# Row maxima of attention: own keys' banks through ScalarE and GpSimd, the maxima's row last in a first score, and the attention output rounded two tiles ahead

## The reference

```python
h = layernorm(x) * (1 + ca) + sa
q = rmsnorm(h @ wq_a.T, q_a_ln_w) @ wq_b.T                  # 32 heads, 64 plain + 64 rotary
ckv, k_pe = h @ wkv_a.T                                      # latent of 32, one rotary key for all heads
k, v = from rmsnorm(ckv) @ wkv_b.T
attn = softmax(where(causal, (q . k) * scale, min))          # 1024 x 1024, causal
x = x + ga * ((attn @ v) @ wo.T)
h = layernorm(x) * (1 + cb) + sb
x = x + gb * ((silu(h @ gate_w.T * s) * (h @ up_w.T * s)) @ down_w.T * s)
```

## Time and profile before

| | |
|---|---|
| median of 3 runs (range) | 802.64 us (801.94 to 804.55) |
| the profiled execution's own time | 803.38 us |
| its span, first to last instruction | 801.60 us |
| mean granted TensorE clock | 0.993 of 2.4 GHz |
| busy: PE, weight loads, DVE, ACT, POOL | 756.7, 494.5, 555.4, 275.2, 156.3 us |
| one of the windows 0 to 5 | 60.9 us each, 6 of them |

### The profile page before, as it was taken

One profiled execution on the slowest core, in us unless ns is written; L12 is line 12 of the kernel. 1 busy time (PEld: TensorE's weight loads), 2 busy tenths in 40 slices (PEclk: granted clock), 3 DMA queues, 4 the chain that ended last, 5 costly groups with the idle time before them and its releaser, 6 DMA issues.

```text
span 801.6 us, 10308 instructions
## 1 busy us (share of the span) xinstructions
PE 756.7 (94%) x3901; PEld 494.5 (62%) x3901; DVE 555.4 (69%) x831; ACT 275.2 (34%) x394; POOL 156.3 (19%) x134
## 2 busy tenths in 40 slices
PE   3898899999999999999999999999799999999998
PEld 1755465555555555565565556545487888887886
DVE  6878579889889889879879878689567323322342
ACT  3732134333333433433333333434344322222210
POOL 1135413113114114114114100022143000000111
PEclk9999899999999999999999999999999999999999
DMA  8433513213213213123123082152100132200011
GB/s 308 159 79 80 133 42 79 65 32 79 55 41 80 49 47 79 42 54 79 35 61 80 15 287 120 59 206 82 51 0 27 51 108 79 73 11 0 27 40 39
DMA packets 36288, 60.72 MB, mean 76 GB/s; under 512 B 4272, under 2 KB 16560, under 8 KB 34448
## 3 DMA queue, kind: packets, MB, share of 16 engines
q1 hardware_dynamic: 36240, 60.06, 26.9%
HBM read 32.66 MB, written 2.10 MB: 43 GB/s over the span
## 4 chain that ended last, share of the span: by engine, by line
PE 58%; DVE 31%; issue 6%; ACT 2%; POOL 2%; DMA 1%; SPq 0%; DVEq 0%; ACTq 0%; POOLq 0%
PE PS L799 15%; DVE PR L1323 8%; PE PS L816 7%; DVE NMa L1226 7%; PE PS L636 5%; PE PS L699 5%; PE PS L714 4%; PE PS L761 4%; PE PS L700 4%; PE PS L701 4%; DVE NMb L1226 3%; DVE wide L1323 3%; PE PS L652 2%; PE PS L626 1%; PE PS L703 1%
## 5 line engine op out<-in xcount | busy, mean ns | idle before, releaser
L965 ACT ACTIVATE PR<-PS 128x1024 f32<-128x1024 f32 (+1 forms) x144 | 132.9, 929 | 259.6 <-PE PS L701 232.3
L1226 DVE TENSOR_REDUCE NMa<-PS 128x1 f32<-128x512 f32 (+3 forms) x216 | 137.8, 660 | 34.3 <-PE PS L640 30.9
L636 PE MATMUL PS<-KH,Q 96*128 96x512 f32 (+3 forms) x384 | 130.6, 400 | 3.5 <-DVE TQ L1211 1.5
L699 PE MATMUL PS<-Q,KH 97*128 97x512 f32 x288 | 130.7, 454 | 0.0
L1323 DVE TENSOR_TENSOR PR<-PR 128x2048 f32<-128x2048 f32 (+3 forms) x56 | 112.5, 2009 | 6.9 <-ACT PR L965 5.5
L700 PE MATMUL PS<-Q,KL 96*128 96x512 f32 x288 | 114.2, 396 | 0.0
L701 PE MATMUL PS<-Q,KH 96*128 96x512 f32 x288 | 113.6, 395 | 0.0
L636 PEld LDWEIGHTS PS<-KH,Q 96*128 96x128 f32 x384 | 67.7, 191 | 56.0 <-issue 29.2
L714 PE MATMUL PS<-PR,V 128*32 128x512 f32 (+3 forms) x704 | 70.4, 488 | 1.7 <-ACT PR L965 1.7
L699 PEld LDWEIGHTS PS<-Q,KH 97*128 97x128 f32 x288 | 55.9, 194 | 25.6 <-issue 13.7
L1441 DVE SCALAR_TENSOR_TENSOR wide<-PS,ffn_s,TQ 128x1024 f32<-128x1024 f32 x10 | 12.8, 1283 | 71.9 <-PE PS L799 71.9
(11 more groups left out here) (185 smaller groups left out, 1060.1 us busy)
## 6 DMA issues: line engine op xcount, KB each, us to landing
Q<-TQ SPq DMA_DIRECT2D x64, 384.0 KB, 5.5
RT<-in_wo SPq DMA_DIRECT2D x4, 1024.0 KB, 4.8
TQ<-in_wo SPq DMA_DIRECT2D x4, 1024.0 KB, 5.8
WI<-in_gate_w SPq DMA_DIRECT2D x10, 256.0 KB, 3.4
WI<-in_up_w SPq DMA_DIRECT2D x10, 256.0 KB, 3.9
DI<-in_down_w SPq DMA_DIRECT2D x10, 256.0 KB, 2.7
PR<-in_wmod_c SPq DMA_DIRECT2D x2, 1024.0 KB, 6.9
x_in<-in_x SPq DMA_DIRECT2D x8, 256.0 KB, 9.7
```

Source lines behind the costliest of these rows:

```text
L636: ins = pe.matmul(bank[:, i * w:(i + 1) * w], M.Q[0:KR, g % 2, 0, qt // 4, h0 + i, qs], M.KH[0:KR, lo:lo + w], start=(i == 0), stop=(i == ...
L699: pe.matmul(dst, M.KH[0:KR + 1, ks], M.Q[0:KR + 1, w % 2, 0, qb, :, qs], start=True, stop=False)
L965: act.activation(tiles, banks, ACT.Exp).then_inc(S_.p, 1)
L1226: dve.tensor_reduce(dst, PS[:, bank_of(turn), 0:n * w].rearrange("p (h k) -> p h k", k=w), axis=AX.X, op=ALU.max, negate=True).then_inc(S_ ...
```

## The change

1. **Own keys' banks.** Of each query tile `qt`, the 128 keys of its own tile (the diagonal block) become a part of their own: 4 heads x 128 columns in one bank. ACT copies it to `diag` in SBUF and frees the bank, POOL sets the masked entries with `affine_select`, and DVE reduces it from SBUF into NMd (`diagonal_reduced`), placed at least three parts behind. The mask matmuls L640 are gone. There are still 38 parts a group: 30 over earlier keys and 8 own ones. `join` takes two minima; it stands two units earlier than `rows` in the windows' table.
2. **First score.** In the first unit of a window the matmul with the maxima's row is issued last, and the wait for the transfer stands ahead of it alone.
3. **Rotary sum in place** (RE is now RT rows 0 and 3), so that the next half's first product waits for `split_low` (`tl`) where it waited for the sum (`re`). WV has a buffer of its own.
4. **Rounding.** AL is made by DVE for all tiles; tiles 0 and 1 after the last add, tile `st + 2` behind the gate of tile `st`. The term with AL comes last, and the first term of tile 1 is issued ahead of the last of tile 0. Four of the modulation columns move out of window 7, to DVE's queue behind the last inverted sums. ACT loads the square root's table ahead.
5. **Last output tile.** Both halves of the last residual are added by DVE.
6. **Group 0.** `FIRST_MAXIMA` puts one piece of group 1's queries behind each own-keys part.

```diff
+    for qt in (3, 2, 1, 4, 5, 6, 7):
+        for lo in range(0, qt * P, 512):
+            w = min(512, qt * P - lo)
...
+        qt = len(parts) - 1 - k
+        if qt < NS and k >= 2 + qt * (len(earlier) - 5) / NS:
+            parts.append((qt, qt * P, P, 0, HG))
```

```diff
-        if diagonal:
-            corner = bank[:, 0:n * w].rearrange("p (h k) -> p h k", k=w)[:, :, w - P:]
-            ins = pe.matmul(corner, M.identb[:], M.maskb[:].unsqueeze(1).broadcast_to([P, n, P]), start=False, stop=True)
...
+    def diagonal_copied(g, k):
...
+        if NS * g + qt >= 2:
+            act.wait_ge(S_.dm, NS * g + qt - 1)
+        act.wait_ge(S_.side, turn + 1)
+        act.activation(M.diag[:, qt % 2].rearrange("p h k -> p (h k)"), PS[:, bank_of(turn), :], ACT.Copy).then_inc(
+            S_.free[turn % 3], 1)
...
+    def diagonal_reduced(g, qt):
+        dve.wait_ge(S_.ds, NS * g + qt + 1)
+        dve.tensor_reduce(M.NMd[:, qt // 4, :, qt % 4], M.diag[:, qt % 2], axis=AX.X, op=ALU.max,
+                          negate=True).then_inc(S_.dm, 1)
...
+        pool.wait_ge(S_.free[TURN[("part", g, k)] % 3], freed(("part", g, k)))
+        pool.affine_select(out=tile, in_=tile, compare_op=ALU.is_ge, fill=MASKED, base=0, pattern=[[0, HG], [-1, P]],
+                           channel_multiplier=1).then_inc(S_.ds, 1)
...
+        dve.tensor_tensor(M.NMj[:], M.NMa[:], M.NMd[:], ALU.min).then_inc(S_.nm, 1)
```

```diff
-        if s == 0 and i == 0:
-            pe.wait_ge(S_.nd, 16 * (w + 1))
...
+        if first:
+
+            pe.wait_ge(S_.nd, 16 * (w + 1))
+            ins = pe.matmul(dst, M.KH[0:KR + 1, ks], M.Q[0:KR + 1, w % 2, 0, qb, :, qs], start=False, stop=True)
```

```diff
-            pe.wait_ge(S_.al, st + 1)
+            pe.wait_ge(S_.ah, st + 1)
...
-        a, w = ((M.AH, M.MH), (M.AL, M.MH), (M.AH, M.ML))[n]
+        if n == 2:
+            pe.wait_ge(S_.al, st + 1)
+        a, w = ((M.AH, M.MH), (M.AH, M.ML), (M.AL, M.MH))[n]
...
+    product_term(1, 0)
...
+    attn_low(0)
+    attn_low(1)
     sums_copied(G - 1, 1)
     invert(G - 1, 1)
-    dve.wait_ge(S_.al, 2)
+    for d in range(KD):
+        mod_late(3, d)
     for st in range(NS - 1):
-        if 2 <= st + 1:
-            attn_low(st + 1)
         gated(st)
+        if st + 2 < NS:
+            attn_low(st + 2)
```

More of the change, by code:

```diff
@@ L333 @@
 SLACK = 0.04
+LEAST_BEHIND = 3
 def maxima_places(begin, end):
-    cost = [0.14 + w * n / 960 for _, _, w, _, n in PARTS]
-    places = [(begin + (end - begin) * sum(cost[:k]) / sum(cost), ("part", k), cost[k]) for k in range(len(PARTS))]
-    return places + [(end + 0.02, ("join",), 0.1), (end + 0.07, ("rows",), 0.3)]
+    cost = [0.35 if is_diagonal(k) else 0.14 + PARTS[k][2] * PARTS[k][4] / 960 for k in range(len(PARTS))]
+    diagonals = [k for k in range(len(PARTS)) if is_diagonal(k)]
+    at = lambda k: begin + (end - begin) * sum(cost[:k]) / sum(cost)
+    places = []
+    for k in range(len(PARTS)):
+        for qt, d in enumerate(diagonals):
+            if k == min(d + LEAST_BEHIND + 1, (diagonals + [len(PARTS)] * 2)[qt + 2]):
+                places.append((at(k), ("least", qt), 0.65))
+        places.append((at(k), ("part", k), 0.0 if is_diagonal(k) else cost[k]))
+    return places + [(end + 0.02, ("join",), 0.1), (end + 0.12, ("rows",), 0.3)]
 def group_places(g, places):
@@ L396 @@
 FIRST_MAXIMA = [("modrow", 0, 1)]
-FIRST_MAXIMA += [key for _, key, _ in sorted(group_places(0, maxima_places(0.04, 0.84)) + group_places(1, QUERY_PLACES),
-                                             key=lambda x: x[0])]
+HANDED_PIECES = [piece for hf in range(2)
+                 for piece in ([("even", 1, hf)], [("odd", 1, hf)], [("lat", 1, hf), ("sum", 1, hf)], [("split", 1, hf)])]
+for key in [key for _, key, _ in sorted(group_places(0, maxima_places(0.0, 0.9)), key=lambda x: x[0])]:
+    FIRST_MAXIMA.append(key)
+    if key == ("part", 0, 1):
+        FIRST_MAXIMA.append(("w", 1))
+    if key[0] == "part" and is_diagonal(key[2]):
+        FIRST_MAXIMA += HANDED_PIECES[PARTS[key[2]][0]]
 BANKED = ("w", "even", "odd", "lat", "part", "rows", "den", "fold", "modrow")
@@ L537, in sp_program @@
         sp.dma_start(out[st * P:(st + 1) * P, :], M.OT[:, st % 2]).then_inc(S_.st[st % 2], 16)
[L539 to L543, removed]
+    for half in range(2):
+        cols = slice(half * D // 2, (half + 1) * D // 2)
+        sp.wait_ge(S_.oh, half + 1)
+        sp.dma_start(out[(NS - 1) * P:NS * P, cols], M.OT[:, 1, cols]).then_inc(S_.st[1], 16)
     sp.wait_ge(S_.nd, 16 * G)
@@ L645, in maxima_rows @@
         pe.wait_ge(S_.nm, g + 1)
[L646 removed]
+        pe.transpose(bank[0:HG * NS, 0:P], M.NMj[:].rearrange("p f h n -> p (f h n)"), M.ident[:]).then_inc(S_.side, 1)
     def denominator(w, qb):
@@ L785, in pe_program @@
     for st in range(1, NS):
-        for n in range(3):
+        for n in range(1 if st == 1 else 0, 3):
             product_term(st, n)
@@ L935, in side @@
             split_high(key[1], key[2])
+        elif key[0] == "part" and is_diagonal(key[2]):
+            diagonal_copied(key[1], key[2])
         elif key[0] == "high":
@@ L1293, in side @@
             split_low_first(key[2])
-        elif kind == "part":
+        elif kind == "part" and not is_diagonal(key[2]):
             part_reduced(g, key[2])
+        elif kind == "least":
+            diagonal_reduced(g, key[2])
         elif kind == "join":
@@ L1565, in side @@
             weights_low(g)
+        elif kind == "part" and is_diagonal(key[2]):
+            diagonal(g, key[2])
         elif kind == "even" and g in HANDED:
@@ L1613, in pool_program @@
                        ALU.subtract).then_inc(S_.lo2, 1)
-    for st in range(NS):
+    for st in range(NS - 1):
         b = st % 2
```

123 lines of the change are left out of this document (67 added, 56 removed).

## The result

| | before | after |
|---|---|---|
| median (range) | 802.70 us (801.94 to 804.55), 4 runs | 790.31 us (787.96 to 791.95), 4 runs |
| ratio, 95% interval | | 0.984, [0.981, 0.987] |
| profiled execution: own time, span | 803.38, 801.6 us | 790.46, 788.2 us |

The change brings 12.4 us, where 5.6 were forecast (802.64 to 797.0).

The account below looks back on a forecast made before the run. No engine fills the window; the chain alternates between DVE and PE, stalling at their hand-over. Terms -6.0 - 5.3 - 0.5 + 2.8 + 1.7 + 1.5 = -5.8 gave about 797.0 us median, range 790.5 to 804.0.

Parts of the forecast that it names:

- The minima ahead of the add: At the window hand-over, PE's 1.02 us wait for a minimum goes in windows 0 to 5: -6.0 us.
- Row last: In a window's first score, waiting later for the row's transfer gains nothing itself but covers the other gains.
- The cap of 1.8 a window: At a window's start, the row's landing lets the first unit start at most about 1.8 us earlier.
- Own keys' banks: At the hand-over, ACT's copies free banks outside DVE's queue: -0.8 us for six windows, -0.5 for window 6, -5.3 total.
- PE's work: In PE's phase, removed masks slightly outweigh added narrower matmuls: -0.2 us a group, -0.5 over the run.
- POOL's masks: In the windows, eight masks of 0.9 us on POOL hold up DVE's adds: +0.4 us a window, +2.8 total.
- Group 0's list: Ahead of the windows, POOL becomes the bound through group 1's queries and eight masks: +1.7 us.
- End of window 7 and first tiles: Behind the windows, a later first gate idles PE some 7 us and the clock falls: +1.5 us together.
- What was to show it: Signs: no transpose waits, windows about 59.3 us, adds over 2.5 us more than twice a window, PE idle 6 us.
- Only the minima help: Rival: PE's bank waits are no bottleneck at the hand-over, so the 5.3 us is lost: 802.5; chance 0.16.
- better than forecast: Rival: masks hit no add and the first tile's gate comes as early as PE's gains allow: 791; chance 0.14.
- The stall is given back: Rival: PE's gains at the hand-over are waited for again in DVE's phase: 808; chance 0.09.

## Why the prediction was right or wrong

- **The minima ahead of the add, -6.0.** Right: -5.3 alone and -6.3 with the row last, in windows 0 to 6.
- **Row last, nothing by itself, the cover of the rest.** Right in kind: 0.1 a window beside the minimum alone, 0.75 in the changed kernel.
- **The cap of 1.8 a window** was wrong. It kept the add, and with it the row, at its old time and let only TensorE come earlier. In a periodic schedule the parts, the reductions and the add come earlier with TensorE; the windows gained 2.65. What is bounded is the distance from the transposes to the row's landing (4.3 us) against that to the row's matmul (4.35).
- **Own keys' banks, -0.8 a window, -5.3 in all.** Right in kind, too large in sum: the copies by ACT are worth 0.65 in a middle window (59.6 to 58.95), but 2.5 over windows 0 to 6 (406.1 to 403.6).
- **PE's work, -0.2 a group, -0.5 in all.** This is the term that failed. It let the masks that leave TensorE and the narrower matmuls that come in nearly cancel. The runs show 0.2 a window for the new list with eight masks in place of 22 (59.8 to 59.6; the rotary sum in place and the parts' places are in this step too), and 0.75 for taking these eight to POOL, locks included. That is 0.95 a window, and 7.4 over windows 0 to 6 (1.4 and 6.0). Two things were mis-sized. First the price: 0.148 us for a matmul of 128 columns came from the one row of four such matmuls behind the denominators (0.59). In the changed kernel 28 of the 80 groups of four stand behind matmuls of the values or denominators and take 0.59; most others take 0.40. The mean of those that wait for nothing is 0.48, or 0.12 a matmul, just below the lower bound of 0.128 that the forecast allowed, and 32 more of them a group were by this estimate 0.9 us too dear. Second the masks: the eight of the own keys vanished in the net sum, though four of them lie on the chain of a window when TensorE makes them, 0.96 us together.
- **POOL's masks, +0.4 a window, +2.8 in all.** Wrong by its size: at most 0.14 a window on the adds. A mask takes 0.63 alone, where 0.9 was taken. It seldom meets an add: 58 of the 64 take 0.6, and the six others, one a window, are themselves held up (1.77 at 203.04, under an add). The Trainium skill, "SBUF — State Buffer", section "Who interferes with whom", says that the ports which DVE and POOL share are an exclusive lock, and that the order of issue decides who blocks; the trace agrees in both directions (an add of 3.40 behind `split_low`, a `split_low` of 3.41 behind an add). The forecast used that rule against the adds alone.
- **Together** the terms of the own keys (copies, PE's work, POOL's masks) were -5.3 - 0.5 + 2.8 = -3.0 by the forecast and -9.9 by the runs (407.5 to 397.6). The 6.9 between them is about the whole miss, 6.7 between forecast and median; what the other terms missed nearly cancels. Some luck is in these sums: window 0 gave 2.2 of the 9.9, and in three kernels with the same code up to there it came out between 55.9 and 56.6.
- **Group 0's list, +1.7.** The sign was right: 32.2 us against 31.4, +0.8, with masks of 0.63.
- **End of window 7 and first tiles, +1.5.** Right in sign and about in size: +1.9 alone, +0.5 within the change. The idle of 7 us was 6.37, and the fall of the clock came.
- **What was to show it.** No wait of the transposes in windows 0 to 5, the idle between the products and the later first window (94.1 against 91.8) came as said. Windows of 59.3 were 58.2, and adds of over 2.5 us were fewer than said: one of four a window, 3.40.
- **The rivals.** "Only the minima help" should read 802.3 by its own sum, not 802.5. The 791 of "better than forecast" is the time that came, but only half of its reasons: masks that hit hardly an add, yes; the first tile's gate no earlier. "The stall is given back" did not come; only the own keys' path without the minimum's move gave part of its gain back, 0.7 a window.

Not settled: why a wait of 1.75 us was followed by a lower clock in four windows and not in two; why window 0 came out so differently between the kernels (54.9 to 58.4 with the own keys' path); and what the rotary sum in place, which the forecast put at nothing, and the parts' earlier places do, which no run has alone.

## What to carry to other kernels

Where a schedule repeats, price a move by the distance between two events of the same period, not by the old time of one of them, and expect parts to be worth more together than alone when one removes the wait that would eat the gain of the other. Take the price of a short instruction from several places, and of instructions that leave an engine count those on the chain, not their net sum with what comes in. Before a long piece of shared-port work is moved away from an add, look at what stands behind it in its own queue: the same move lost 2 us ahead of a 0.63 us mask and won 6 us behind it.

## What the runs showed of the hardware

- A wait of TensorE of 1.75 us, in otherwise full work, was followed by a granted clock of 0.55, nearly its lower level of 1.2 GHz, for 3.7 us in four of six windows (1.00 in the other two); the waits of 1.02 in the kernel before never were. Beyond the wait itself it cost 1.5 us each time. Near the end of window 7 the same holds from run to run: an idle time of 1.70 was followed by 0.60 and 0.55 in the kernel before, and by 1.00 in the kernel with the minimum alone.
- A reduction of 512 columns to four takes DVE about as long from SBUF (675 ns) as from PSUM (686 ns, in the kernel without copies), so a copy by another engine gains it nothing but its place in the queue.
- Four matmuls of 96 rows and 128 columns take 0.40 us in the chain, 0.59 directly behind those of the values or denominators (weights of 128 x 32); a mask of 512 columns takes 0.63 on POOL, 0.23 to 0.25 as a matmul.
